# Identity products between TensorE's work, the convolution begun behind two semaphores, and the weight splits moved to its middle pairs

## What is computed

```
z = rmsnorm(u, pre_norm_w) @ in_proj_w.T            # 768 channels
z = causal depthwise convolution of 3 taps + bias
x2, x1, v = split(z);  xv = x1 * v
h = sum_s residues * exp(log_poles * t)             # long filter, 16 poles a channel
y = (fft_conv(xv, h) + xv * D_skip) * x2
y = y @ out_proj_w.T + u
y = y + (gelu(rmsnorm(y) @ l1_w.T) * (rmsnorm(y) @ l2_w.T)) @ l3_w.T
x = layernorm(x + y)
x = layernorm(x + attention(x) + cross attention)   # 16 heads, causal; projection Wp
x = layernorm(x + low-rank ffn(x))                  # U1 V1 gelu U2 V2
```

## Time and profile before

| | |
|---|---|
| median of 3 runs | 2197.38 us (2192.62 to 2197.82) |
| profiled execution, its own time | 2197.36 us |
| its span, first to last instruction | 2195.6 us |
| mean granted clock | 0.965 |
| busy: PE, DVE, ACT, POOL | 1985.4, 1468.2, 1222.3, 883.2 us |
| project, longconv, mlp, attend, ffn begin at | 0.8, 217.7, 287.2, 783.9, 1977.9 us |

### The profile page before, as it was taken

The page is one execution under the profiler, slowest core; times in us unless marked ns, Lnnn a source line. Parts: engine busy times, 40 slices in busy tenths (PEclk is TensorE's granted clock), DMA queues, the critical chain, the costliest instruction groups (busy, mean ns, idle before and its releaser), DMA issues. The chain is left out here.

```text
span 2195.6 us, 39396 instructions
## 1 busy us (share of the span) xinstructions
PE 1985.4 (90%) x12897; PEld 1348.4 (61%) x12960; DVE 1468.2 (67%) x2652; ACT 1222.3 (56%) x2425; POOL 883.2 (40%) x1336
## 2 busy tenths in 40 slices
PE   6786949999999868999999999999999999968997
PEld 4665337888888755566566665566655665535554
DVE  6898634555555427777778777777777787724776
ACT  6775535555555423665656656565656556645554
POOL 3443615555555431334333434344333433332222
PEclk9999969999999979999999999999999999978999
DMA  3343121211122244343443344342443334112221
GB/s 116 123 149 125 44 77 68 77 68 69 67 73 76 78 106 91 77 106 72 104 105 85 79 93 103 92 103 64 109 103 80 90 81 94 43 39 66 78 87 66
DMA packets 104787, 188.10 MB, mean 86 GB/s; under 512 B 27961, under 2 KB 78137, under 8 KB 98489
## 3 DMA queue, kind: packets, MB, share of 16 engines
q1 hardware_dynamic: 104632, 186.13, 31.7%
HBM read 110.23 MB, written 58.79 MB: 77 GB/s over the span
## 5 line engine op out<-in xcount | busy, mean ns | idle before, releaser
L1516 ACT ACTIVATE at_pt<-at_ps_w 128x512 f32<-128x512 f32 x640 | 377.8, 598 | 232.8 <-PE at_ps_w L1392 232.7
L1743 DVE TENSOR_REDUCE at_mneg<-at_ps_s 128x1 f32<-128x384 f32 (+3 forms) x704 | 437.3, 636 | 94.9 <-PE at_ps_s L1381 87.3
L1606 POOL TENSOR_SCALAR_AFFINE_SELECT at_pt<-at_pt 128x256 f32<-128x256 f32 (+1 forms) x640 | 233.5, 368 | 576.3 <-ACT at_pt L1516 573.8
L1380 PE MATMUL at_ps_s<-at_ks,at_qs 96*128 96x128 bf16 (+3 forms) x1024 | 259.4, 306 | 25.0 <-DVE at_mneg L1743 22.7
L1392 PE MATMUL at_ps_w<-at_qs,at_ks 97*128 97x512 bf16 (+3 forms) x1024 | 244.3, 301 | 9.0 <-ACT at_pt L1516 5.0
L1380 PEld LDWEIGHTS at_ps_s<-at_ks,at_qs 96*128 96x128 bf16 x1024 | 86.2, 99 | 215.1 <-DVE at_mneg L1743 140.5
L895 POOL TENSOR_TENSOR ml_m_lo<-ml_m,ml_m_hi 128x512 fp32r<-128x512 f32 x80 | 115.9, 1450 | 181.0 <-ACT ml_m_hi L801 180.7
L1408 PE MATMUL at_ps_o<-at_pt,at_val 128*32 128x512 f32 (+3 forms) x2048 | 169.1, 449 | 9.7 <-POOL at_pt L1606 9.5
L1381 PE MATMUL at_ps_s<-at_mask,at_ident 128*128 128x128 bf16 (+1 forms) x641 | 149.4, 233 | 0.0
L834 ACT ACTIVATE ml_gl<-ml_ps_g 128x512 f32<-128x512 f32 x96 | 56.7, 591 | 153.8 <-PE ml_ps_u L127 150.0
L1392 PEld LDWEIGHTS at_ps_w<-at_qs,at_ks 97*128 97x128 bf16 x1024 | 88.3, 98 | 62.9 <-ACT at_pt L1516 14.8
(11 more groups left out here) (255 smaller groups left out, 5582.3 us busy)
## 6 DMA issues: line engine op xcount, KB each, us to landing
parts_d<-at_parts SPq DMA_DIRECT2D x64, 384.0 KB, 2.5
at_ks<-parts_d SPq DMA_DIRECT2D x192, 128.0 KB, 7.8
at_qs<-parts_d SPq DMA_DIRECT2D x32, 384.0 KB, 5.7
pj_xin<-in_x SPq DMA_DIRECT2D x16, 512.0 KB, 5.3
gate_d<-pj_zc SPq DMA_DIRECT2D x16, 512.0 KB, 2.7
xv_all<-pj_turned_xv SPq DMA_DIRECT2D x16, 512.0 KB, 4.2
ml_turned_y<-xv_all SPq DMA_DIRECT2D x16, 512.0 KB, 3.4
ml_x<-gate_d SPq DMA_DIRECT2D x16, 512.0 KB, 4.3
```

Source lines behind the costliest of these rows:

```text
L1380: pe.matmul(out[:, i, :], qs[par][0:ROWS, h, toks], ks[par][0:ROWS, h, 0:(qt + 1) * P], start=i == 0, stop=False)
L1516: act.activation(pt[u % RING][:], ps_w[u % 2][:], ACT.Exp, scale=SCALE).then_inc(exped, 1)
L1606: pool.affine_select(out=diag, in_=diag, compare_op=ALU.is_ge, fill=0.0, base=0, pattern=pattern, channel_multiplier=-1).then_inc(cut, 1)
L1743: dve.tensor_reduce(mneg[:, g, h0 % HG:h0 % HG + count, qt], view_score(ps_s[s % 2], qt, count), AX_X, ALU.max, negate=True).then_inc(maxe ...
```

## The change

Six groups of edits. (1) `keep_running` issues `count` float32 products of the identity with itself into a PSUM bank that is free there: 26 at the end of `project`; 42 before `out_product(0)`, 24 before and 8 after `turn(0)`, 24 before the last `down` and 32 after it in `mlp`; in `attend` 6 after job t1 and 16 after k0 in step -2, 6 after r3 in the last step, 5 before y0 and 5 before p0 in the tail, 30 at its end; 6 after each of the first two `turn` in `ffn`. (2) `project` no longer waits at its end for the stores; TensorE waits for those of `xv_all` before its first `gather`, SP for those of `x2` before it loads weights. (3) The semaphores of `project` are kept open (`held`) and set back by SP in `longconv` after the first gather; the seven of `longconv` are set back by SP at the end of `mlp`. (4) `store` issues the `xv_all` store ahead of the `x2` store. (5) `WEIGHTS` becomes one weight each at pairs 8, 12, 16, 20 and 24. (6) Signatures follow.

```diff
+def keep_running(pe, out, square, count):
+    for _ in range(count):
+        pe.matmul(out, square, square, start=True, stop=True)
...
             def store(b, par):
+                sp.wait_ge(chunked, KT * (b + 1))
+                sp.dma_start(xv_all[...], turned_xv[par][...]).then_inc(placed[par], 16)
                 sp.wait_ge(tap0_done, CT * (b + 1))
                 sp.dma_start(x2_d[...], zc[par][:, 0:KT, :]).then_inc(x2_stored[par], 16)
-                sp.wait_ge(chunked, KT * (b + 1))
-                sp.dma_start(xv_all[...], turned_xv[par][...]).then_inc(placed[par], 16)
...
-            for i in range(2):
-                sp.wait_ge(x2_stored[i], 16 * (B // 2))
-                sp.wait_ge(placed[i], 16 * (B // 2))
             sp.wait_ge(f.filt_in, 16 * C)
...
             over_late(pe, B, step)
+            keep_running(pe, ps_t[:, 0, 0:P], ident[:], 26)
...
-        WEIGHTS = {NP - 4: (0, 1), NP - 3: (2, 3), NP - 2: (4,)}
+        WEIGHTS = {8: (0,), 12: (1,), 16: (2,), 20: (3,), 24: (4,)}
...
         def _(sp):
+            for i in range(2):
+                sp.wait_ge(held.of(f"x2_stored{i}"), 16 * (B // 2))
...
+            sp.wait_ge(gathered, 1)
+            for semaphore in held.semaphores:
+                sp.sem_clear(semaphore)
...
+            for i in range(2):
+                pe.wait_ge(held.of(f"placed{i}"), 16 * (B // 2))
             gather(0, 0)
...
             store(B - 1)
+            for semaphore in spent:
+                sp.sem_clear(semaphore)
...
+            keep_running(pe, ps_g[1][:, 0:P], ident[:], 42)
             out_product(0)
+            keep_running(pe, ps_g[1][:, 0:P], ident[:], 24)
             turn(0)
+            keep_running(pe, ps_g[1][:, 0:P], ident[:], 8)
...
             over(pe, B, step)
+            keep_running(pe, ps_u[1][:, 0:P], ident[:], 24)
             down(B - 1, 1)
+            keep_running(pe, ps_u[1][:, 0:P], ident[:], 32)
...
                         job(name, of_batch(name, b), 1 - par)
+                        if b == -2 and name in RAMP:
+                            keep_running(pe, ps_o[:, 0:P], ident[:], RAMP[name])
+                        if is_last(b) and name in ("r3",):
+                            keep_running(pe, ps_s[0][:, 0:P], ident[:], 6)
...
+                if name in ("y0", "p0"):
+                    keep_running(pe, ps_s[0][:, 0:P], ident[:], 5)
                 job(name, B - 1, 1)
+            keep_running(pe, ps_s[0][:, 0:P], ident[:], 30)
...
+RAMP = {"t1": 6, "k0": 16, "k1": 0}
...
             for k in range(KT):
                 turn(0, 0, k)
+                keep_running(pe, ps_o[:, 0, 0:P], ident[:], 6)
             first(0, 0)
```

More of the change, by code:

```diff
@@ L100, in sem, with of @@
         return self.semaphores[-1]
[L102 to L108, removed]
+    def of(self, name):
+        return next(s for s in self.semaphores if s.name == f"{self.tag}_{name}")
 def group(xv_all, g):
@@ L231, in project @@
             f, lp_rows, lp_cols, res_cols, lp_chan, res_chan, skip, c_left, c_ramp, c_lag, c_qmask, c_hmask, c_gmask, c_notfirst,
-            filt_d):
+            filt_d, held):
     CT = 3 * KT
@@ L260, in project @@
         ps_z = [n.psum(f"ps_z{i}", [P, T]) for i in range(CT)]
[L262 to L265, removed]
+        par_loaded, w_loaded, w_scaled, w_high, w_split = (held.sem(s) for s in ("par_loaded", "w_loaded", "w_scaled", "w_high", "w_split"))
+        x_loaded = [held.sem(f"x_loaded{i}") for i in range(2)]
+        x2_stored = [held.sem(f"x2_stored{i}") for i in range(2)]
+        placed = [held.sem(f"placed{i}") for i in range(2)]
         const_set, squared, ms_set, rstd_set, normed, turned, high_set, low_set = (
-            n.sem(s) for s in ("const_set", "squared", "ms_set", "rstd_set", "normed", "turned", "high_set", "low_set"))
+            held.sem(s) for s in ("const_set", "squared", "ms_set", "rstd_set", "normed", "turned", "high_set", "low_set"))
         z_ready, tap2_done, tap1_done, tap0_done, gated, chunked = (
[L269 to L272, removed]
+            held.sem(s) for s in ("z_ready", "tap2_done", "tap1_done", "tap0_done", "gated", "chunked"))
+        side_set, side_added = held.sem("side_set"), held.sem("side_added")
+        pool_settled = held.sem("pool_settled")
         block = ctx.enter_context(nc.Block())
@@ L282, in store @@
             def store(b, par):
+                sp.wait_ge(chunked, KT * (b + 1))
+                sp.dma_start(xv_all[:, bass.ds(b, 1)].rearrange("p o g n -> p (o g n)"),
+                             turned_xv[par][:].rearrange("p g n -> p (g n)")).then_inc(placed[par], 16)
                 sp.wait_ge(tap0_done, CT * (b + 1))
@@ L285, in store @@
                              zc[par][:, 0:KT, :]).then_inc(x2_stored[par], 16)
-                sp.wait_ge(chunked, KT * (b + 1))
-                sp.dma_start(xv_all[:, bass.ds(b, 1)].rearrange("p o g n -> p (o g n)"),
-                             turned_xv[par][:].rearrange("p g n -> p (g n)")).then_inc(placed[par], 16)
             def load_filters():
@@ L526, in _, with longconv @@
             over_late(dve, B, step)
-def longconv(nc, f, xv_all, gw, w_out, w_gate, w_up, w_tail, w_down, w_scale, c_ident):
+def longconv(nc, f, xv_all, gw, w_out, w_gate, w_up, w_tail, w_down, w_scale, c_ident, held):
     NP = G // 2
@@ L671, in _, with mlp @@
             over_pairs(dve, step)
-def mlp(nc, x, x2_d, gw, xv_all, x1_d, early, c_ident, c_heads, w_qkcv, w_ctx, w_proj, b_qkc, b_ck, b_rows, ctx_t):
+    return n.semaphores
+def mlp(nc, spent, x, x2_d, gw, xv_all, x1_d, early, c_ident, c_heads, w_qkcv, w_ctx, w_proj, b_qkc, b_ck, b_rows, ctx_t):
     with ExitStack() as ctx:
@@ L2043, in decoder_layer @@
                     f = Filters(nc, filters)
+                    held = Names(nc, filters, "pj")
                     project(nc, a["x"], a["w_in"], a["pre_w"], a["taps"], a["tap_bias"], a["c_ident"], xv_all, gate_d,
                             f, a["lp_rows"], a["lp_cols"], a["res_cols"], a["lp_chan"], a["res_chan"], a["skip"], a["c_left"],
-                            a["c_ramp"], a["c_lag"], a["c_qmask"], a["c_hmask"], a["c_gmask"], a["c_notfirst"], filt_d)
+                            a["c_ramp"], a["c_lag"], a["c_qmask"], a["c_hmask"], a["c_gmask"], a["c_notfirst"], filt_d, held)
                     gw = GatedWeights(nc, gated)
-                    longconv(nc, f, xv_all, gw, a["w_out"], a["w_gate"], a["w_up"], a["w_tail"], a["w_down"], a["post_w"], a["c_ident"])
-                mlp(nc, a["x"], gate_d, gw, xv_all, x1_d, early, a["c_ident"], a["c_heads"], a["w_qkcv"], a["w_ctx"], a["w_proj"],
+                    spent = longconv(nc, f, xv_all, gw, a["w_out"], a["w_gate"], a["w_up"], a["w_tail"], a["w_down"], a["post_w"], a["c_ident"], held)
+                mlp(nc, spent, a["x"], gate_d, gw, xv_all, x1_d, early, a["c_ident"], a["c_heads"], a["w_qkcv"], a["w_ctx"], a["w_proj"],
                     a["b_qkc"], a["b_ck"], a["b_rows"], a["ctx_t"])
```

## The result

The changed kernel takes 2200.74 us (median of 9, 2198.16 to 2206.62), the kernel before 2194.95 beside it (9 runs, 2192.62 to 2201.23). The ratio is 1.0027, 95% interval [1.0016, 1.0038]: 5.8 us slower. 2204.4 was forecast, 2187 to 2211. The profiled execution took 2198.95 us, span 2197.2, so 1.6 us more span than the one of before.

What follows compares the result with a forecast made beforehand. TensorE, busy for 90% of the span, was taken as the bound. Mlp's later start +6.1, its start +1.5, its end +1.2, attend's start -1.8, its end +2.8 and ffn -2.8 make +7.0: 2204.4 us, range 2187 to 2211.

Steps and rivals of the forecast that it cites:

- The price of a product: For each 128-column identity product: 0.33 us at full clock, on a line between 64 columns (0.11) and 256 (0.27).
- one of the two signs by which the prediction called itself wrong: Wrong if mlp begins before 287, or if identity products end before the work they stand in front of is ready.
- Project's end: From project to the first gather: the xv_all store lands before the identity products end, gather at 215.45, -2.7 us.
- Mlp's start: At mlp's start: 42 products end 3.5 us late, out_product at full clock gives back 2.5; in sum +1.5 us.
- Attend's end and the products behind it: Attend's tail is +0.6 us late, and its 30 last products overfill the wait by +2.2; +2.8 in all.
- The splits: Weight splits moved to convolution pairs 8 to 24: stalls +12.7 us, half clock behind three long ones +5.4; -6.8 off the end.
- First pairs at full clock: At the convolution's start: the first pairs run at full instead of mostly half clock, -2.5 us.
- Attend's start: At attend's start: warm transposes and q0 save 1.8 us, the other products fit the waits; -1.8 (0 to -3).
- rival A: At all seams: cheap products of 0.22 us end inside the rests, so the time is 2191 us; chance 0.22.
- B: Rival, in the convolution: VectorE takes the splits in, 12.7 and 5.4 fall away, 2186 us; chance 0.12.
- C: Rival, in the convolution: the stalls come but the clock holds, 2199 us; chance 0.13.
- D: Rival, at the identity products: they don't hold the clock, or run at half of it; 2215 us or more; chance 0.08.

## Why the prediction came out, step by step

**The price of a product: wrong.** I took 0.33 us; it is 0.22. The step that failed is the line between 64 and 256 columns (0.11 and 0.27), at both ends. The 0.27 is the product at 837.58, the one exception: in the other fifteen of this shape in the same trace, as at 901.67, the two instructions start 0.22 apart, and the identity products of 256 columns measured 0.216.

```profile
901.67 0.60 PE L1323 MATMUL at_ps_j<-ea_wc,ea_ctx 128*128 128x256 f32 x2
```

And the 0.11 at 64 columns is a floor, not a point of the line: 128 take 0.112 too, half of 256. The argument against the cheap price (64 columns took 0.11 and not 0.06) was right as a row and wrong as a reason, since what those rows showed was that floor. The figure of rule A from the Trainium skill ("TensorE: Matmul & The Clock Gate", Back-to-back issue gap, with the four passes of "FP8 and Floating Point Precision", TensorE Precision Notes) came true at 128 columns, by estimate 0.22 and measured 0.22; at 64 columns the same rule gives 0.12 a product and 0.22 was measured. The same section calls this the gap of a product alone and puts a stream of weight loads and products at about 81 ns for one of 128 columns; that would be 0.32 for four by estimate, my price almost, and the measured 0.22 speaks against it. With my price the seams came out too dear.

Project's end: -4.3 for -2.7. Here the overlap was wrong too: I had the `xv_all` store land before the products end, and it landed after them; the gather waited for it, and came 8.0 us behind project's last product with identity products and 7.9 to 8.0 without. Mlp's start: the products ended at 308.6, 2.6 us ahead of the first product behind them and not 3.5 us after its inputs, which is one of the two signs by which the prediction called itself wrong; the first product still came 2.1 late, by the load, and with the rest (-1.7 for -2.0) the sum was +0.35 for +1.5. Mlp's end up to down's last product: -2.3 for -1.3. Attend's end and the products behind it: -4.1 for +2.8. The +2.2 in it for the last 30 products was nothing: they took 6.9 us and fit the 8.06 to ffn's first turn, which is the same in both kernels. The rest of the -4.1 is not shown to be the products' at all, as this stretch varies by 8 us among kernels with the same products (1150.9 to 1158.9).

**The splits: right in kind, too small.** Five gaps in front of the gather, as forecast, four of them followed or met by half clock, where I had it behind the three long ones. The term was 12.7 + 5.4 = 18.1; it measured 23.1. Stalls are 1.8, 3.8, 3.8, 1.8 and 4.2, 15.5 together, for 1.4, 3.3, 3.3, 1.4 and 3.3: behind the low part of the three large ones L640 came 2.2 to 2.3 us later and not 1.7, since the gather in the gap already ran at half clock (1.05 for 0.58), and wd's was the dearest. At wo the gather ran at full clock, and the 0.4 are a low part of 0.92 for 0.69 and an L640 1.9 behind it. Half clock behind them is 7.6 for 5.4: it fell at four of the five, the small wt's too. Off the end they took 6.5 for my 6.8.

**First pairs at full clock:** -3.1 for -2.5; against the two otherwise equal kernels without products 1.8 to 2.0. **Attend's start:** -1.3 here, for -1.8; against kernels without products 2.3 to 2.5. **Ffn:** 2.5 at its start, 3.5 in all, for 2.8; against those two kernels 2.1 to 2.2 in all.

**What I didn't see.** The instruction packet in the way of mlp's first load, +2.1 and gone again with other code ahead of it. And the seven clears, which I hid behind TensorE: they stand behind the last store on SP, and the block ends with SP, so +0.7 whatever TensorE does.

Put together: my own sum for the cheap product was -6.3. With what the splits cost more (+5.0 in the middle, +0.3 at the end), the load (+2.1) and the clears (+0.7) it is +1.8, and the two profiled spans differ by 1.6. That these two agree so well is chance again: project's later end (+2.3) and an mlp start that gave 1.5 less than rival A had were made up for by attend's end, 3.7 better than in A for no shown reason. The medians differ by 5.8, since the profiled execution of before is one of its slower and that of the change one of its faster ones. So the forecast's +7.0 came near the measured +5.8 by luck, with a price 13 us too dear against 8 us that weren't seen. Of the rivals, A had the products right and the time wrong (2191), as it kept 18.1 for the splits and knew no late load. B, C and D fell with the profile: the stalls came, the clock fell behind four of the five, and it stood at 1.00 through the identity products at project's end and mlp's start. (In four of the later runs some of mlp's 42, or of their wider stand-ins, ran at 0.50. In one of these, the changed kernel with the old table, they were in the way: the inputs were ready 11.6 us behind the load and the first product came at 12.5.)

## What to carry to other kernels

When work is slipped into a pipelined loop, its busy time matters less than what stands behind its wait: the same 36.9 us on VectorE cost 23 us with the low part one pair behind the high part that it waits for, and 1.5 with it three behind. Filling TensorE's rests with idle products pays where the rest is longer than they are and full work follows (2.9 us from 26 products in mlp), and not where the next wait is another engine's (attend's start). When two terms of a forecast are uncertain and of opposite sign, a hit on the total proves neither.

## What the runs showed of the hardware

- A plain float32 product with a 128x128 left side is two instructions, at full clock of 0.11 us at 64 and at 128 columns, 0.22 at 256 and 0.43 at 512.
- Behind 26 products of 64 columns at that same spacing the clock fell to 0.50 at 214.3, in one profile; behind 26 of 128 it stayed at 1.00 through the first pairs, in six.
- In the five kernels with a 16 KB packet of the instruction queue, 1 us long, in the middle of mlp's first 512 KB loads, the inputs of the first product were ready 1.3 to 2.2 us later than in the seven without.
- A semaphore clear on SP is 0.06 us at the end of a block, and seven of them with what goes with them 0.7.
